# Where the second half of a block's silu activations runs on ScalarE, in a two-layer fp32 sequence kernel

## What is computed

```
x = layernorm(x + L0_attn(x)); x = layernorm(x + L0_ffn(x))
# L1_attn, D=256 channels, 16 states
x_ssm, z = split(x @ w_in.T + b_in);  z = silu(z)
dt = softplus(x_ssm @ w_dt.T + b_dt); Bm, Cm = x_ssm @ w_B.T + b_B, x_ssm @ w_C.T + b_C
for each state n:  h = exp(A[:, n] * dt) * h + dt * Bm[n] * x_ssm;  y += h * Cm[n]
y = ((y + D * x_ssm) * z) @ w_out.T + b_out;  x = layernorm(layernorm(y + x) * gamma + beta)
# L1_ffn, 256 -> 1024 -> 256
y = silu(layernorm(x) @ w1 + fc1_bias);  x = layernorm(x + 0.5 * (y @ w2 + fc2_bias))
```

## Time and profile before

| | |
|---|---|
| median of 3 runs | 1148.7 us |
| the profiled execution's own time | 1148.39 us |
| its span, first to last instruction | 1146.6 us |
| PE busy over the span | 1021.7 us (89%) |
| DVE busy | 924.9 us (81%) |
| ACT busy | 840.9 us (73%) |
| POOL busy | 701.7 us (61%) |
| from one block's first silu to the next block's | 67.7 us, five times; then the end |

### The profile page before, as it was taken

How to read it: one execution, slowest core, us unless ns; L and a number is a source line. 1 busy time by engine, 2 the same in 40 slices (tenths; PEclk the granted TensorE clock), 3 DMA queues, 4 the chain that set the end, 5 groups by cost and what they waited for, 6 DMA issues and landing times. The chain is left out here.

```text
span 1146.6 us, 17126 instructions
## 1 busy us (share of the span) xinstructions
PE 1021.7 (89%) x5234; PEld 701.9 (61%) x5234; DVE 924.9 (81%) x1166; ACT 840.9 (73%) x1641; POOL 701.7 (61%) x623
## 2 busy tenths in 40 slices
PE   6999999999879999995648699999999999988887
PEld 4777777777643344443436367576676766756576
DVE  7999999999824665453799898999999999999741
ACT  7868878887634456556667789898988989896843
POOL 3466656775721453353666868778697886968420
PEclk9999999999979999998788799999999999999999
DMA  6534443443232011114755455546555675656201
GB/s 184 148 120 134 116 123 112 134 116 114 85 108 78 1 37 44 48 55 107 209 143 166 115 167 129 150 132 156 154 132 168 139 161 137 152 136 140 70 9 37
DMA packets 93230, 133.81 MB, mean 117 GB/s; under 512 B 8786, under 2 KB 47698, under 8 KB 93140
## 3 DMA queue, kind: packets, MB, share of 16 engines
q1 hardware_dynamic: 93140, 132.73, 42.5%
HBM read 116.45 MB, written 14.16 MB: 114 GB/s over the span
## 5 line engine op out<-in xcount | busy, mean ns | idle before, releaser
L2197 DVE TENSOR_TENSOR_SCAN state<-bank_a,h,state 128x512 f32<-128x512 f32 x256 | 316.0, 1269 | 34.0 <-POOL state L2405 12.2
L2405 POOL TENSOR_TENSOR state<-uc,Bb 128x1024 f32<-128x1024 f32 x64 | 151.0, 2369 | 61.7 <-DVE prod L2203 36.6
L2405 POOL TENSOR_TENSOR state<-s,Bb 128x1024 f32<-128x1024 f32 x64 | 151.0, 2369 | 49.4 <-DVE prod L2203 33.6
L1655 PE MATMUL bank_y<-ident,prod 128*128 128x128 f32 x1024 | 139.3, 283 | 30.5 <-DVE prod L2203 30.5
L1655 PEld LDWEIGHTS bank_y<-ident,prod 128*128 128x128 f32 x1024 | 123.9, 147 | 69.0 <-DVE prod L2203 36.9
L2203 DVE TENSOR_TENSOR prod<-state,bank_c 128x1024 f32<-128x1024 f32 x128 | 154.0, 1203 | 6.4 <-ACT bank_c L1876 4.4
L1700 PE MATMUL bank_m<-w,f_h 128*128 128x256 f32 x448 | 104.5, 383 | 0.0
L40 PE MATMUL bank_m<-nT,w 128*128 128x512 f32 x224 | 102.0, 593 | 0.9 <-ACT nT L1938 0.9
L1871 ACT ACTIVATE bank_a<-dtc,A 128x512 f32<-128x512 f32 x128 | 86.6, 682 | 18.0 <-DVE state L2197 14.3
L1871 ACT ACTIVATE bank_a<-s,A 128x512 f32<-128x512 f32 x128 | 86.2, 680 | 11.8 <-DVE state L2197 11.6
L1700 PEld LDWEIGHTS bank_m<-w,f_h 128*128 128x128 f32 x448 | 84.7, 193 | 13.1 <-issue 2.4
(11 more groups left out here) (365 smaller groups left out, 2444.3 us busy)
## 6 DMA issues: line engine op xcount, KB each, us to landing
Bb<-CB_rows SPq DMA_DIRECT2D x128, 256.0 KB, 4.2
Cb<-CB_rows SPq DMA_DIRECT2D x128, 256.0 KB, 4.6
abc<-decays SPq DMA_DIRECT2D x32, 512.0 KB, 4.6
Ebc<-ramps SPq DMA_DIRECT2D x64, 128.0 KB, 3.2
uT<-in_uT SPq DMA_DIRECT2D x8, 512.0 KB, 4.5
u<-in_u SPq DMA_DIRECT2D x8, 512.0 KB, 4.0
x_tokens<-x2s SPq DMA_DIRECT2D x8, 512.0 KB, 2.9
x_rows<-x1T SPq DMA_DIRECT2D x8, 512.0 KB, 2.7
```

The costliest lines, as they stand in the source:

```text
L1655: i = e.matmul(p_y[c // 2][:, at:at + P], prod[n % 2][:, k, c * CH:(c + 1) * CH], ident[:, :], start=False, stop=(n == NS - 1), is_transpo ...
L2197: e.tensor_tensor_scan(s[:, k, :], p_a[k][:, :], s[:, k, :], h0[:, n, k:k + 1], ALU.mult, ALU.add).then_inc(v_s, 1)
L2405: e.tensor_tensor(state[at % 3][:, :, :], uc[b % 2][:, :, :], both(Bb[n % 4][:, :]), ALU.mult).then_inc(p_b, 1)
```

## The change

In ACT's loop `silu_up(last, 2)` and `silu_up(last, 3)` move from the first silu stretch of a block to a place some 17 steps later, behind `spread_C(cur, 4)`. `silu_z` and `spread_C(cur, 2)` stay. `decay(cur, 6, 0)` is moved ahead of `norm3(post, 0)`. In PE's `down_proj` the one wait for all four silus becomes two waits: half 0 of chunk 0 waits for the first two silus, half 1 of chunk 0 for all four. The guard holds for the blocks 0 to 5 (`last < NB - 2`), six in all; the silus of block 6, after the loop, are left as they are.

```diff
                 def down_proj(b, c, half):
                     to = pair[c // 2][:, (c % 2) * DM:(c % 2 + 1) * DM]
+                    if c == 0:
+                        e.wait_ge(a_fs, 4 * b + 2 * half + 2)
                     if half == 0:
-                        if c == 0:
-                            e.wait_ge(a_fs, 4 * b + 4)
                         if c % 2 == 0:
...
                     if 0 <= last < NB - 2:
                         silu_up(last, 0)
                         silu_up(last, 1)
-                        silu_up(last, 2)
                     if live(cur):
                         silu_z(cur)
                         spread_C(cur, 2)
-                    if 0 <= last < NB - 2:
-                        silu_up(last, 3)
-                    if live(cur):
                         decay(cur, 4, 0)
                         carry(cur, 2)
...
                         carry(cur, 4)
                         decay(cur, 5, 1)
                         spread_C(cur, 4)
+                    if 0 <= last < NB - 2:
+                        silu_up(last, 2)
+                        silu_up(last, 3)
+                    if live(cur):
+                        decay(cur, 6, 0)
                     if 0 <= post < NB - 1:
                         norm3(post, 0)
                     if live(cur):
-                        decay(cur, 6, 0)
                         spread_C(cur, 5)
                     if 0 <= post < NB - 1:
                         norm3(post, 1)
```

## The result

The changed kernel takes 1157.64 us (median of 4 runs, 1156.39 to 1158.75) and the kernel before, run beside it, 1148.15 us (4 runs, 1146.68 to 1149.27). The ratio is 1.0082 with a 95% interval of 1.0067 to 1.0098: slower by 0.8%, or 9.5 us. The profiled execution of the changed kernel took 1156.39 us, its span is 1154.6 us.

A forecast was written before the change was run, and what follows sets the result against it. No engine alone was the bound, but a chain of waits from ACT's silu stretch over POOL's norm45 to xn and PE. Five blocks at 1.51 us plus 1.0 gave 8.6 on 1148.39: 1157.0 us, range 1151 to 1165.

The forecast's parts named there:

- The stretches on ACT: ACT's two silu stretches per block: decay 4 comes 1.93 us sooner, norm3(1) 2.74 us later.
- PE: Down projection: the 1.34 us wait before half 0 goes, 2.7 us come before half 1; second d_proj 1.37 us late.
- DVE: Scans: no 1.81 us wait before scan 4, about 3.0 us before scan 6, then about 1.9 us late.
- POOL and `xn`: Deciding term: scaled waits for norm3(1); 2.74 us less slack and semaphore time makes scaled, xn and block end 1.51 late.
- the walk: Last of six changed blocks: norm3(1) about 2.1 us late, POOL slack 1.3, xn 0.8 us late; 1.0 taken.
- The cost of a load: ACT's table loads around the silus: 1.28 us each, 1.30 from its start to the next start, no drain.
- The rival of the costly switch: ACT empties around each switch, at twice the load's 1.28 us: scaled 4.1 us late, 1173 us; chance 0.02.
- The clock: PE after its new 2.7 us wait before half 1: the clock was taken to stay at the higher level.
- the rival: Clock falls after PE's new wait: matmuls 3.42 not 1.89 us, product 5 held 0.9; 0.5 a block, 1160; chance 0.08.

The follow-up runs named there:

- The kernel with decay 6 ahead (and `add_up(3)` too): Changed kernel with decay 6 half 0 before the second silu stretch and, on PE, add_up(3) before down_proj of chunk 0 half 1: 1155.39 us, ratio 1.0056.
- the kernel in which the clock stayed up: Changed kernel with only add_up(3) moved on PE ahead of down_proj of chunk 0, half 1: 1157.92 us, ratio 1.0080.
- Identity activations: Changed kernel with Identity in place of Silu in the two moved activations, so no table loads around them: 1142.81 us, ratio 0.9959.
- with decay 6 ahead: Changed kernel with decay 6 of half 0 moved ahead of the second silu stretch, load back behind both norm3: 1162.5 us, ratio 1.0127.
- the second dose: Changed kernel with a one-column Exp between the two moved silus, bringing two more table loads: 1179.36 us, ratio 1.0270.

## Why the prediction was right

The forecast of 1157.0 us was met within 0.6 us, and most of its steps can be read off the trace of the changed kernel one by one. That the totals lie so close is partly luck, since the runs of the changed kernel alone scatter over 2.4 us; the delay itself was forecast at 8.6 us and measured at 9.5.

- **The stretches on ACT.** Decay 4 was to come 1.93 us sooner and `norm3(1)` 2.74 us later than before. Counted from the first load they came at 6.04 (7.97 before) and at 18.78 (16.00): 1.93 and 2.78.
- **PE.** No wait before half 0, and 2.7 us before half 1; it was 2.52. The gain was put at nothing since the next wait takes its place, and the split wait alone (ratio 1.0001) showed this.
- **DVE.** Some 3.0 us before scan 6, measured 2.95; 1.9 us late from the second half of scan 6 on, measured 1.99. Here the working fell short in one respect. I followed DVE's delay only as far as the question whether POOL's inputs come in time and gave it no price of its own. The kernel with decay 6 ahead (and `add_up(3)` too) shows it to be worth 1.0 us a block with the way over `norm3` nearly repaired. In the changed kernel it lies beside the 1.6 us and doesn't add to them. Product 5 was put at 840.7, which is 18.9 after the first load: it came at 18.93 in the block shown, but at 19.8 to 20.1 in the other four, by the clock (below).
- **POOL and `xn`.** `scaled` 1.51 us late: measured 1.66, and 1.62 at `turn_normed`. This is the term of the sum that was a little small. Over the five blocks it was 1.75 a block and not 1.51, which makes 1.2 us of the result; of the 1.75, the kernel in which the clock stayed up keeps 1.65. In the last block the walk gave 0.8 and I took 1.0; it was 0.7.
- **The cost of a load.** 1.28 us and nothing around it, by the earlier trace rows. In the changed kernel the silu starts 1.29 us after its load and decay 6 1.29 us after the second one. The rival of the costly switch asked for `scaled` to be 4.1 us late. The Trainium skill ("ScalarE: Activation LUTs", What ACT_TABLE_LOAD costs) would add a drain of some 1380 ns to each switch; no run here shows one, and the 2.5 us a block (2.8 in the full ones) that the pair of loads cost against Identity activations leaves no room for two of them beside the loads' own 2.56. The same page's advice (Rules for kernel authors), to group by function set, holds: the spreading alone was a gain of 5.2 us, and the loads turned it into a loss.
- **The clock.** I took it that the granted clock would stay at the higher level after the new wait. It did so in the block that I have shown, but in the five blocks the eight matmuls behind the wait took 2.78, 3.57, 1.99, 2.84 and 3.46 us. So this assumption was wrong in four of five blocks, and that the forecast held all the same is luck: more slack than I had counted took it up. Product 5 did wait 1.1 to 1.3 us for `add_up(3)` in these four blocks, as the rival said. But PE still had 0.1 to 0.4 us left before `xn`, and DVE's lateness was used up before the gate, all but 0.1 us a block: the kernel with `add_up(3)` ahead, in which the matmuls ran at the higher level in all five blocks, has 69.32 for 69.42. My rival priced it at 0.5 us a block. Where product 5 is early, as with decay 6 ahead, it costs up to 3 us a block.

The last block was judged by a coarse walk, and it came out at +0.7. There PE waits 6.49 us before half 1, for the 5.8 that I had estimated:

```profile
1046.66 3.38 PE L1700 MATMUL bank_m<-w,f_h 128*128 128x256 f32 x8 [6.49 <-ACT f_h L1949]
```

What stays open: why the fourth block is 0.2 to 0.3 us longer than the others (69.68, and 69.56 with `add_up(3)` ahead), and why the level of the clock differs from block to block behind waits of the same length.

## What to carry to other kernels

A wait that is taken away is worth nothing until the next thing from the same source is looked up: here PE's 1.34 us before the down projection and its 1.21 before the next projection both ended with one stretch on ACT. Splitting a batch of activations of one table set puts a load at each end of the new part; follow what is queued behind it to each engine that waits, subtract each one's slack once, and expect the second dose to pass whole. And look at what stands in a long stretch's shadow without needing it: moving one 0.2 us instruction out of it gained some 4 us, against the 5 that spreading the silus would have given without loads, probably much the same microseconds.

## What the runs showed of the hardware

- A table load takes 1.28 us in a dense queue, with 0.01 to 0.02 us between it and its activation, whether one or four stand within 8 us. Norms and row copies (Identity, Copy) ran between a silu and the load back without a load of their own: with decay 6 ahead, both `norm3`, `spread_C(5)` and a `carry`.
- The granted clock behind a wait of PE within otherwise dense work was not the same from block to block. In the full blocks, after waits of 1.1 to 1.65 us the matmuls ran at the higher level. The eight of the down projection took 1.99 to 3.57 us after 2.26 us, 1.99 to 3.61 after 2.52, 2.00 to 3.78 after 3.13, and 3.46 or 3.78 after 5.44. At the higher of the two levels, 2.4 GHz, they take 1.89 us; 3.78 is twice that, 1.2 GHz.
- What such a lower clock cost was set by what stood behind it in PE's queue and by the slack there: 0.10 us a block in the changed kernel, 1.3 to 3 us with decay 6 early and `add_up(3)` behind those matmuls, 0.3 to 0.5 with `add_up(3)` ahead of them.
